# Order of the expert rows in DRAM, and the count of idle products, in a macaron block with top-4 of 32 experts

## The reference

```python
x = x + 0.5 * _L0_ffn_ref(_layernorm(x), ...)
x = x + _L0_attn_ref(_layernorm(x), ...)
x = x + 0.5 * _L0_ffn_ref(_layernorm(x), ...)

# _L0_ffn_ref: rmsnorm, router, top 4 of 32 experts, then for each token and chosen expert
h1 = einsum('th,efh->tef', tf, w1) + b1                   # 128 -> 256
glu = minimum(h[..., ::2], 7.0); lin = clip(h[..., 1::2], -7.0, 7.0)
h = glu * sigmoid(1.702 * glu) * (lin + 1.0)
out = einsum('tef,ehf->th', h * combine, w2) + combine @ b2   # 128 -> 128

# _L0_attn_ref: q and k are softmaxes over the width, 16 heads of 8, no softmax over the scores:
# probs = scores / sum(scores), ctx = probs @ v
```

## Time and profile before

| | us |
|---|---|
| median of 3 runs | 726.69 |
| the three runs | 727.34, 726.69, 723.95 |
| the profiled execution | 724.5 |
| its span, first to last instruction | 722.8 |
| granted TensorE clock, mean share of full speed | 0.842 |

### The profile page before, as it was taken

The page is one execution under the profiler, slowest core; times in us unless marked ns, Lnnn a source line. Parts: engine busy times, 40 slices in busy tenths (PEclk is TensorE's granted clock), DMA queues, the critical chain, the costliest instruction groups (busy, mean ns, idle before and its releaser), DMA issues.

```text
span 722.8 us, 12887 instructions
## 1 busy us (share of the span) xinstructions
PE 525.7 (73%) x3232; PEld 443.3 (61%) x3235; DVE 437.0 (60%) x1243; ACT 347.9 (48%) x752; POOL 505.3 (70%) x551
## 2 busy tenths in 40 slices
PE   6258887999999998395607864999999999834000
PEld 3154266999898997163504552699989999734000
DVE  7889223555457778388993877255555767744222
ACT  4444414666566665495607743366656666511000
POOL 3677777777437777777677777777752777777765
PEclk9557999999999999697558955999999999967555
DMA  7997115666556664221111111466655666424222
GB/s 267 390 382 287 54 52 166 199 198 197 177 164 196 199 197 154 64 55 53 48 51 55 51 52 54 137 199 208 203 183 161 197 199 204 153 72 126 65 63 57
DMA packets 56491, 108.26 MB, mean 150 GB/s; under 512 B 12576, under 2 KB 19968, under 8 KB 56320
## 3 DMA queue, kind: packets, MB, share of 16 engines
q1 hardware_dynamic: 40064, 74.13, 30.9%
q0 software_dynamic: 16384, 33.59, 16.1%
HBM read 51.00 MB, written 56.62 MB: 149 GB/s over the span
## 4 chain that ended last, share of the span: by engine, by line
PE 48%; POOL 17%; DVE 13%; issue 11%; ACT 6%; DMA 4%; POOLq 0%; DVEq 0%; ACTq 0%; SPq 0%
PE PS L1242 19%; PE PS L1137 11%; PE PS L1255 10%; POOL xs L535 10%; POOL YG L560 6%; ACT swish L668 3%; PE PS L1356 2%; DMA xrow<-xs 2%; DVE PS L986 1%; DMA xs<-U,row 1%; DMA YG<-ys,row 1%; PE PS L1342 1%; DVE st L717 1%; PE PS L1317 1%; DVE chosen L777 1%
## 5 line engine op out<-in xcount | busy, mean ns | idle before, releaser
L560 POOL DMA_INDIRECT YG<-ys,row x256 | 245.5, 959 | 117.7 <-issue 77.5
L535 POOL DMA_INDIRECT xs<-U,row x256 | 249.4, 974 | 81.9 <-issue 73.2
L1242 PE MATMUL PS<-W,xT 128*128 x768 | 183.1, 381 | 0.2 <-DVE glulin L931 0.2
L1242 PEld LDWEIGHTS PS<-W,xT 128*128 128x128 f32 x768 | 139.0, 191 | 16.1 <-issue 0.9
L931 DVE TENSOR_SCALAR glulin<-PS 128x512 f32<-128x512 f32 x96 | 66.4, 691 | 127.8 <-PE PS L1255 100.0
L625 ACT ACTIVATE yrow<-PS 128x512 f32<-128x512 f32 x96 | 57.3, 597 | 108.7 <-PE PS L1255 108.7
L1255 PEld LDWEIGHTS PS<-W,hidT 128*128 128x128 f32 x768 | 99.9, 191 | 14.4 <-issue 10.0
L1255 PE MATMUL PS<-W,hidT 128*128 x768 | 102.3, 276 | 7.0 <-ACT hidT L633 6.9
L944 DVE SCALAR_TENSOR_TENSOR hid<-glulin,swish 128x512 f32<-128x512 f32 x96 | 66.7, 694 | 15.9 <-ACT swish L629 15.2
L637 ACT ACTIVATE xT<-PS 128x512 f32<-128x512 f32 x96 | 56.5, 589 | 38.8 <-PE PS L1137 38.8
L629 ACT ACTIVATE swish<-glulin 128x512 f32<-128x512 f32 x96 | 60.5, 630 | 22.3 <-DVE glulin L931 14.1
(11 more groups left out here) (178 smaller groups left out, 710.3 us busy)
## 6 DMA issues: line engine op xcount, KB each, us to landing
xrow<-xs SPq DMA_DIRECT2D x96, 256.0 KB
ys<-yrow SPq DMA_DIRECT2D x96, 256.0 KB, 2.2
xs<-YG SPq DMA_DIRECT2D x6, 2048.0 KB, 13.4
W<-in_w12T SPq DMA_DIRECT2D x1, 6144.0 KB
xs<-U,row POOLq DMA_INDIRECT x256
YG<-ys,row POOLq DMA_INDIRECT x256
out<-X SPq DMA_DIRECT2D x7, 256.0 KB, 2.5
X<-in_x SPq DMA_DIRECT2D x4, 256.0 KB, 3.7
```

Source lines behind the costliest of these rows:

```text
L535: pool.indirect_dma_start(out=xs[c], out_offset=bass.IndirectOffsetOnAxis(ap=row[:, i:i + 1], axis=0), in_=U[:, (c * CT + t) * H:(c * CT + ...
L560: pool.indirect_dma_start(out=YG[:, t * TOPK + k, :], out_offset=None, in_=ys[c], in_offset=bass.IndirectOffsetOnAxis(ap=row[:, i:i + 1], ...
L1242: last = te.matmul(h1, xT[:, s, q * P:(q + 1) * P], W[:, bass.ds(es[q], 2 * H)], start=True, stop=True)
```

## The change

1. The views of xs and ys become "(g q p) h": the row in DRAM is the place itself. A load and a store now have, for each partition, four runs of 512 bytes in place of one of 2048. The amount, the count of DMAs and their issuing queue stay.
2. The four operations of slots_to_rows go, with their tiles; the reduction of L829 writes `row` and raises `rows_ready` itself.
3. NIDLE_E goes from (18, 34) to (38, 34): 20 more idle products ahead of the first pass.

```diff
-NIDLE_E = (18, 34)
+NIDLE_E = (38, 34)
...
-        pos = sb("pos", [P, PAIRS], I32)
-        pos_a = sb("pos_a", [P, PAIRS], I32)
-        pos_b = sb("pos_b", [P, PAIRS], I32)
...
-        xs_v = [a.rearrange("(g p q) h -> g p (q h)", p=P, q=GT) for a in xs]
-        ys_v = [a.rearrange("(g p q) h -> g p (q h)", p=P, q=GT) for a in ys]
+        xs_v = [a.rearrange("(g n) h -> g n h", n=GT * P) for a in xs]
+        ys_v = [a.rearrange("(g q p) h -> g p q h", p=P, q=GT) for a in ys]
...
-                    sp.dma_start(xrow[:, r, :], xs_v[c][bass.ds(k, 1)].rearrange("g p n -> (g p) n"))\
+                    rows = xs_v[c][bass.ds(k, 1)].rearrange("g n h -> (g n) h")
+                    sp.dma_start(xrow[:, r, :].rearrange("p (q h) -> p q h", h=H), rows.rearrange("(q p) h -> p q h", p=P))\
                         .then_inc(xrow_loaded[r], 16)
...
-                    sp.dma_start(ys_v[c][bass.ds(k, 1)].rearrange("g p n -> (g p) n"), yrow[:, r, :])\
+                    sp.dma_start(ys_v[c][bass.ds(k, 1)].rearrange("g p q h -> (g p) q h"),
+                                 yrow[:, r, :].rearrange("p (q h) -> p q h", h=H))\
                         .then_inc(yrow_stored[r], 16)
...
-                        link(v.tensor_reduce(pos[:, pr], pl.rearrange("p (t e) -> p t e", e=NE), X_AXIS, ALU.add))
-
-                def slots_to_rows(first, stop):
-
-                    pr = slice(first * TOPK, stop * TOPK)
-                    linked[0] += 1
-                    v.tensor_scalar(pos_a[:, pr], pos[:, pr], P - 1, None, ALU.bitwise_and).then_inc(chain, 1)
-                    link(v.tensor_scalar(pos_b[:, pr], pos[:, pr], 7, GT - 1, ALU.logical_shift_right, ALU.bitwise_and))
-                    link(v.scalar_tensor_tensor(pos_a[:, pr], pos_a[:, pr], float(GT - 1), pos[:, pr], ALU.mult, ALU.add))
-                    v.scalar_tensor_tensor(row[:, c * PAIRS + first * TOPK:c * PAIRS + stop * TOPK], pos_b[:, pr],
-                                           float(1 - P), pos_a[:, pr], ALU.mult, ALU.add).then_inc(rows_ready, stop - first)
+                        v.tensor_reduce(row[:, c * PAIRS + first * TOPK:c * PAIRS + stop * TOPK],
+                                        pl.rearrange("p (t e) -> p t e", e=NE), X_AXIS, ALU.add)\
+                            .then_inc(rows_ready, n)
```

More of the change, by code:

```diff
@@ L848, in end @@
                     v.tensor_scalar(ended[:], slot_no[:], span[:, 0:1], None, ALU.is_ge).then_inc(ended_ready, 1)
-                def rows(first, stop):
-                    slots(first, stop)
-                    slots_to_rows(first, stop)
                 if c == NCHUNK - 1:
@@ L857, in route @@
                     tile_experts()
-                    rows(0, GT)
+                    slots(0, GT)
                 elif ph == 0:
                     begins(0, 1)
-                    rows(0, 1)
+                    slots(0, 1)
                     begins(1, CT)
-                    rows(1, GT)
+                    slots(1, GT)
                     end()
@@ L881, in weights @@
                                                 ALU.mult, ALU.mult))
-                return slots, slots_to_rows, weights
+                return slots, weights
             def split(src, rest, dst):
@@ L1070, in _ @@
                     stats(c * CT + t, c)
-                slots, slots_to_rows, weights = route(c, c)
+                slots, weights = route(c, c)
                 slots(GT, CT)
-                slots_to_rows(GT, CT)
                 weights()
@@ L1114, in _ @@
             attention(0, NCHUNK)
-            slots, slots_to_rows, weights = route(NCHUNK, NCHUNK + 1, lambda: combine(NCHUNK - 1, CTB, CTB + 6))
+            slots, weights = route(NCHUNK, NCHUNK + 1, lambda: combine(NCHUNK - 1, CTB, CTB + 6))
             slots(GT, CT)
-            slots_to_rows(GT, CT)
             weights()
@@ L1120, in _ @@
             attention(1, NCHUNK + 2)
-            slots, slots_to_rows, weights = route(NCHUNK + 1, NCHUNK + 3)
+            slots, weights = route(NCHUNK + 1, NCHUNK + 3)
             slots(GT, CT)
-            slots_to_rows(GT, CT)
             weights()
```

## The result

The changed kernel took 732.3 us (median of 6 runs, 731.4 to 734.3) against 725.5 (723.5 to 727.3) for the kernel before on the same chip: ratio 1.009 [1.0066, 1.0114], 6.9 us slower. The stated range of 8 in 10 (723.5 to 734.0) held; the size did not, since 2.4 us had been forecast. The result lies above the half per cent (up to 730.3) to which the prediction had given 0.63; "slower" had 0.32. The profiled execution of the changed kernel took 732.11 us with a span of 730.4, so it stands at the median, and 7.6 us above the span of before.

The account below looks back on a forecast made before the run. A relay of POOL's scatters and gathers, landings and TensorE's groups bounds the kernel. Terms 0 + 0 + 1.8 + 0.6 = 2.4 us gave 726.9 from the profiled 724.5, or 729.1 from the median 726.69; 8-in-10 range 723.5 to 734.0.

Parts of the forecast that it names:

- Part 1: Removing the four integer operations: 7.1 us of DVE goes, but POOL's own queue covers it, so 0 us.
- rival A: At the hand-over to chunk 1, longer TensorE waits drop the clock: 1.5 us more, 730.6; chance 0.13.
- Part 3: Runs of 512 bytes: 0.3 us more for each load or store, six exposed, plus slower gathers beside the loop.
- 1.8 + 0.6 = 2.4 us: Six exposed transfers at 0.3 us, plus 0.6 us for gathers beside the loop; the whole forecast loss.
- The factor 1.38: Engine time of a 0.262 MB transfer in 512-byte against 2048-byte runs: 0.95 against 0.69 us, 0.26 us more.
- the 1.13: Skill's estimate of the cost of shorter runs from packet overhead: 0.1 us a transfer, 0.6 us for six.
- The forecast of 0.45 us for the fourth gather: First pass: the gather's 1.2 us behind other packets grows by 0.38 with shorter runs, 0.45 us.
- the relay: Sequence setting the end: POOL's scatters and gathers, landings of loads and stores, and TensorE's groups, handing over in turn.
- rival (C): Faster: TensorE's waits vanish and indirect landings shorten, 3.7 us gained, 723.0; POOL's step depends on neither; chance 0.08.
- Idle products, forecast 0: 20 more ahead of the first pass keep the clock up, but the gain goes into TensorE's wait: 0 us.
- the hand-over: At about 195 us TensorE goes to chunk 1 and waits for its first load; wait forecast 1.2 to 2.2 us.
- Rival (B): In the loop the DMA engines fill up (68% plus scatters, 83%) and TensorE starves: 747; with (D) chance 0.14.

Follow-up runs that it names:

- e6: Kernel before with the changed views of xs and ys (runs of 512 bytes), four operations kept, 18 idle products: 729.67 against 727.23 us, ratio 1.0034.
- e10: Kernel before with runs of 512 bytes in the loads only, operations kept, 18 idle products: 725.5 against 725.78 us, ratio 0.9999.
- e11: Kernel before with runs of 512 bytes in the stores only, operations kept, 18 idle products: 729.63 against 725.78 us, ratio 1.0047.
- e8: Changed kernel with 18 idle products ahead of the first pass in place of 38: 731.24 us against 726.73 for before, ratio 1.0065.
- e4: Changed kernel with 18 idle products, on a chip where the kernel before took 863.07 us: ratio 0.9989 to before.
- e7: Kernel before with 38 idle products ahead of the first pass, nothing else: 725.07 against 726.73 us, ratio 0.9982.
- e12: Kernel before with 38 idle products and six more in the step from chunk 0 to chunk 1: 726.04 against 725.78 us, ratio 1.0003.
- e5: Changed kernel with ten more idle products in the step from chunk 0 to chunk 1: 731.62 us against 727.23 for before, ratio 1.006.
- e9: Changed kernel with 18 idle products ahead of the first pass and 46 of the second: 734.22 us against 726.73 for before, ratio 1.01.

## Why the prediction was right or wrong

**The direction was right, the size wrong.** Forecast +2.4 us, measured +6.9. The nine stretches of the table add up to the 7.6 us of the spans: −0.14 + 0.24 + 2.18 + 0.98 + 0.76 + 1.56 + 0.41 + 1.45 + 0.16. Two steps failed: the 0 for the removed operations (Part 1), and leaving the fall of the clock out of the sum (rival A). The price of the runs (Part 3) came out, in part by luck.

**Runs of 512 bytes, forecast 1.8 + 0.6 = 2.4 us: 2.5 [1.5, 3.3] (e6).** The sum is right, its working isn't. The factor 1.38 set a store's stretch against one of loads with the queue full. In the loop SP's queue took 49.6% of the engines for 5.26 MB before and 54.6% for 5.28 after the earlier trace rows, a factor of 1.10; the 1.13 that the prediction worked out and set aside was nearer. It said that loads and stores cost alike; alone, the loads give 0 [−1.5, 1.4] us (e10), which does not exclude the 0.6 forecast for two of them, and the stores 3.4 [2.3, 4.5] (e11), above the 1.8 forecast for stores and gathers. The load at the first hand-over landed in 2.73 us, not in the 2.95 named. The forecast of 0.45 us for the fourth gather seems borne out by 4.29 against 3.68, but e6, with the same runs, has 3.42: that growth goes with the removed operations. The rule of the Trainium skill that was weighed there ("DMA: Bandwidth & Descriptors", section "Specifications", 512 B as the least for line rate) agrees with the loads of e10 beside the scatters and not with the stores of e11.

**Removed operations, forecast 0: about +2.3 us (e8 against e6).** "Nothing on the relay comes earlier" held: the third scatter still stands straight behind a gather with 0.30. The idle products of the second pass began 71.9 us behind the third scatter instead of 74.1, so 2.2 us earlier and not 1.6, and TensorE stood 3.07 us and not 2. But the bound for unknown costs was 0 on the side of a loss. The statement in rival (C) that POOL's step depends on neither edit is one that fell: four more long DMAs at some 0.45 us each are 1.8 us, about what the fourth scatter grew by (1.56). The other loss is in the first pass: a gather that lands later, a longer wait of TensorE and with it the half clock, as told under e8. What sets the number of long DMAs isn't settled; of the kernels on the later chips those without the operations have seven or eight, those with them one to four (on the chip that didn't serve e4, without them, has two).

**Idle products, forecast 0: −1.3 us alone (e7).** The first rows were turned at 113.09 with the clock at 1.00 in 112 to 116, and the gain went into the wait at the hand-over, 0.75 to 1.40, as said. That the median is a little lower all the same was not foreseen and has no place in the profile, whose execution was e7's longest. Within the change (1.009, against 1.0065 for e8) the intervals overlap; whether the idle products help or hurt there is open.

**Rival (A)** described what happened, at about its price. The clock fell where it was said to, behind a wait of 1.40 us, and TensorE needed 15.23 us from turning chunk 1's rows to the first gather, where the kernel before needed 13.44 and the ten such stretches of e6, e8, e10, e11 and e12, none with a fall, 13.11 to 13.69: some 1.7 us, forecast 1.5. On the chips with 726 us every kernel profiled without the operations has such a fall in the first pass, here or behind the first addition (e5, e8, e9), and of those with them only e7. It counts the same microseconds as the runs and operations above, not further ones: it is a way in which a longer wait becomes dearer.

**Rival (B)** did not come. The shares were 54.6 and 15.4, together 70% and not 83. The first rows of chunk 0 and of chunk 1 were turned 83.03 us apart (113.09 to 196.12), before 83.26: the loop didn't stretch. One load on the chain, at 579.68, took 5.94 us, more than the 5.0 that the loop allows, and TensorE stood 0.45 us for it, so the loads in the loop were not wholly hidden, as the prediction had them.

**The parts and the whole.** Loads and stores apart give 0.9999 and 1.0047, both together 1.0034: one and the same within the intervals. With the removed operations 1.0065, with the idle products 1.009. So of 6.9 us some 2.5 come from the short runs, about 2.3 from the removed operations, and the rest, up to 2 us, is within what the intervals leave open. The one kernel found that beats the one before is e7, the kernel before with 38 idle products, by 0.2%.

## What to carry to other kernels

Price a landing by what stands behind it, not by its own growth alone. A rate measured on a store need not hold for a load, nor one at a full queue for a steady loop. Operations that are hidden can still go with a loss, so a term that gains 0 needs a bound on the other side too; where POOL issues DMAs beside DVE, an edit that shifts the one against the other can be worth 0.45 us for each meeting. And before a profile is used to say that an effect costs nothing, look where the profiled execution stands among the others: e7's was its longest.

## What the runs showed of the hardware

An indirect DMA on POOL takes 0.96 us and comes every 1.26, but some take 1.1 to 1.5. Most of these start just behind the start of DVE's multiply of 128x512 (L930 in the changed kernel, 0.69 us, both inputs in SBUF). In the 14 profiles on record 275 indirect DMAs started 0.05 to 0.42 us after such a multiply. Every one took longer, 1.10 to 1.48 us, and every one ended 1.50 to 1.54 us after the multiply's start. Those that started up to 0.3 us ahead of it, or at most 0.04 behind, took at most 1.08; those that started 0.43 to 0.7 us behind, at most 1.10. So the sooner behind its start a DMA begins, the longer it takes, as if held until a fixed moment of the multiply. DMAs that started during an addition (L893, 0.35 us, also from SBUF) and beside no multiply took at most 1.07. The changed kernel in the fourth scatter, POOL first, then DVE:

```profile
506.87 1.41 POOL L534 DMA_INDIRECT xs<-U,row  x1 [0.30 <-issue]
508.59 0.96 POOL L534 DMA_INDIRECT xs<-U,row  x1 [0.30 <-issue]
509.85 0.96 POOL L534 DMA_INDIRECT xs<-U,row  x1 [0.30 <-issue]
511.11 0.96 POOL L534 DMA_INDIRECT xs<-U,row  x1 [0.30 <-issue]
512.38 0.96 POOL L534 DMA_INDIRECT xs<-U,row  x1 [0.30 <-issue]
513.64 1.46 POOL L534 DMA_INDIRECT xs<-U,row  x1 [0.30 <-issue]
```

```profile
506.75 0.69 DVE L930 SCALAR_TENSOR_TENSOR hid<-glulin,swish 128x512 f32<-128x512 f32 x1 [0.27 <-ACT swish L628]
...
510.17 0.69 DVE L930 SCALAR_TENSOR_TENSOR hid<-glulin,swish 128x512 f32<-128x512 f32 x1 [0.19 <-ACT swish L628]
...
513.58 0.69 DVE L930 SCALAR_TENSOR_TENSOR hid<-glulin,swish 128x512 f32<-128x512 f32 x1 [0.19 <-ACT swish L628]
```

The DMAs at 506.87 and 513.64 start 0.12 and 0.06 us into a multiply, take 1.41 and 1.46 us and end 1.53 and 1.52 us after its start; that at 509.85 starts ahead of one and isn't long. A long one pushes POOL back by some 0.45 us. Eight steps of 1.26 and the 0.45 are 10.5 us, three groups of TensorE at 3.49, so the meeting can recur every eight DMAs once the two are in step; here it recurs after five. The Trainium skill ("SBUF — State Buffer", section "SBUF: two separate sides") says that VectorE with two SBUF inputs and a GpSimd operation that reads SBUF shut each other out of a shared pair of ports, whoever starts first. That fits the order of the starts here, if the indirect DMA reads SBUF so, which no run shows. What the section tells of DMAs from GpSimd's queue that are held up, it tells of another kind of VectorE operation. No run here took the multiply away to test it.
